# Value sums of a sampling pipeline moved from TensorE to VectorE, ten gather buffers, and a new product order in the attention that runs beside it

## What is computed

```python
v00, v01, v10, v11 = gather(y0i, x0i), gather(y0i, x1i), gather(y1i, x0i), gather(y1i, x1i)
out = v00 * (1 - wx) * (1 - wy) + v01 * wx * (1 - wy) + v10 * (1 - wx) * wy + v11 * wx * wy
...
attn = jnp.einsum('bgpc,bgpkc->bgpk', qh, k)      # layer 0: 9 samples k of a pixel p and group g
attn = jax.nn.softmax(attn, axis=-1)
out = jnp.einsum('bgpk,bgpkc->bgpc', attn, v)
...
logits = jnp.einsum('bhqd,bhkd->bhqk', q, k) * scale      # layer 1
attn = jax.nn.softmax(logits, axis=-1)
ctx = jnp.einsum('bhqk,bhkd->bhqd', attn, v)
```

## Time and profile before

| | |
|---|---|
| median of 3 runs | 10331.16 us (10326.96 to 10343.2) |
| the profiled execution | 10341.0 us, its span 10339.2 us |
| PE busy | 7631.7 us, 74% of the span |
| DVE busy | 5293.7 us, 51% |
| ACT busy | 3754.9 us, 36% |
| POOL busy | 5133.8 us, 50% |
| mean granted clock of TensorE | 0.858 of full speed |

### The profile page before, as it was taken

How to read it: one execution, slowest core, us unless ns; L and a number is a source line. 1 busy time by engine, 2 the same in 40 slices (tenths; PEclk the granted TensorE clock), 3 DMA queues, 4 the chain that set the end, 5 groups by cost and what they waited for, 6 DMA issues and landing times. The chain is left out here.

```text
span 10339.2 us, 94511 instructions
## 1 busy us (share of the span) xinstructions
PE 7631.7 (74%) x30870; PEld 3966.5 (38%) x30870; DVE 5293.7 (51%) x9576; ACT 3754.9 (36%) x5426; POOL 5133.8 (50%) x4768
## 2 busy tenths in 40 slices
PE   7623326654893799879999687978996999855894
PEld 3612213442442344334444233433442444333563
DVE  7555544564664566556666455656632666421003
ACT  2100002310561366526666244635663455400221
POOL 1078875676776677767777576767500000002003
PEclk9866667877896799979999888988998999966997
DMA  3854335675543555455454445545412111142223
GB/s 128 310 140 107 108 106 162 205 257 178 154 132 117 157 145 140 130 150 147 131 145 134 152 143 159 142 136 154 129 37 77 53 47 46 33 117 93 69 75 108
DMA packets 680981, 1331.69 MB, mean 129 GB/s; under 512 B 173223, under 2 KB 417980, under 8 KB 665376
## 3 DMA queue, kind: packets, MB, share of 16 engines
q0 software_dynamic: 229632, 631.22, 22.0%
q1 hardware_dynamic: 432480, 619.58, 19.5%
q10 hardware_dynamic: 18432, 75.51, 1.8%
HBM read 1018.55 MB, written 307.68 MB: 128 GB/s over the span
## 5 line engine op out<-in xcount | busy, mean ns | idle before, releaser
L660 POOL DMA_INDIRECT sa_slot<-s_table,sa_rec x4608 | 4942.4, 1073 | 2462.7 <-issue 1413.8
L1572 PE MATMUL a_ctx<-a_p,a_v 128*64 128x512 f32 x6400 | 1740.3, 622 | 177.6 <-issue 177.6
L1659 DVE CUSTOM_DVE_ANT_0 a_above<-a_late,a_above 128x512 f32<-128x512 f32 x1600 | 1105.6, 691 | 1449.9 <-PE a_late L1517 1381.0
L1591 ACT ACTIVATE a_p<-a_s 128x1024 f32<-128x1024 f32 x1600 | 1629.9, 1019 | 154.6 <-PE a_s L1555 154.0
L1600 ACT ACTIVATE a_above<-a_diff 128x512 f32<-128x512 f32 x1600 | 956.2, 598 | 1855.9 <-PE a_diff L1505 1820.1
L815 PE MATMUL sa_sums<-keep_ident,sa_vals 128*128 128x128 f32 x4608 | 711.5, 305 | 759.4 <-DVE sa_vals L758 759.4
L1505 PE MATMUL a_diff<-a_kd,a_q 96*128 96x512 f32 x1600 | 840.4, 525 | 277.7 <-DMA a_q<-s_q 256.0
L1555 PE MATMUL a_s<-a_q,a_k 98*128 98x512 f32 x3200 | 1042.6, 407 | 0.0
L815 PEld LDWEIGHTS sa_sums<-keep_ident,sa_vals 128*128 128x128 f32 x4608 | 581.5, 157 | 1171.7 <-DVE sa_vals L758 774.5
L706 DVE TENSOR_TENSOR sa_slot<-sa_slot,sa_q 128x1152 f32<-128x1152 f32 x512 | 693.5, 1354 | 613.7 <-DMA sa_slot<-s_table,sa_rec 613.7
L2155 POOL MEMSET x_ctx<- 128x2 f32 x2 | 0.2, 101 | 1802.2 <-POOLq L74 1802.2
(11 more groups left out here) (272 smaller groups left out, 7922.5 us busy)
## 6 DMA issues: line engine op xcount, KB each, us to landing
sa_slot<-s_table,sa_rec POOLq DMA_INDIRECT x4608
s_table<-t_rows ACTq DMA_DIRECT2D x64, 1024.0 KB, 7.5
a_q<-s_q SPq DMA_DIRECT2D x160, 384.0 KB, 4.4
s_part<-a_o SPq DMA_DIRECT2D x160, 256.0 KB, 2.5
t_qwin<-s_dwq SPq DMA_DIRECT2D x64, 512.0 KB, 6.0
t_kvwin<-s_dwkv SPq DMA_DIRECT2D x64, 386.0 KB, 12.1
a_kd<-s_kd SPq DMA_DIRECT2D x128, 192.0 KB, 4.1
a_o<-s_part SPq DMA_DIRECT2D x96, 256.0 KB, 2.7
```

Of the source, the lines that this page charges most:

```text
L660: pool.indirect_dma_start(out=self.slot[g][:, k, :, :, :].rearrange("p c a n -> p (c a n)"), out_offset=None, in_=self.s["table"][n // TIL ...
L1572: mm = pe.matmul(self.ps_ctx[i * 2 * HD:(i + 1) * 2 * HD, :], self.v_and_ones(run.head, kb), self.p[slot % P_SLOTS][:, i * CHUNK:(i + 1) * ...
L1591: act.activation(self.p[slot % P_SLOTS][:, :], self.ps_s[slot % 2], ACT.Exp, scale=float(HD) ** -0.5).then_inc(self.exped, 1)
L1659: dve.tensor_tensor_reduce(above, self.ps_late, above, 1.0, LOWEST, ALU.add, ALU.max, self.pair_max[:, t, j:j + 1]).then_inc(self.late_got, 1)
```

## The change

Three things are changed together.

- The value products stay on DVE but are written in place, over the values in the gather buffer. A new DVE instruction for each group (`add_values`) sums the 36 corner samples of 32 channels into `vals`, which is now [128, 128] for each half tile. It reads the samples with a pitch of 64 elements (256 bytes) as the inner step. PE keeps one transpose for each half tile (`turn_values`). A half tile becomes 19 pieces and a tile 38, so in slots 0 and up every slot has one piece; the tile rate of one in 38 slots is the same. `PROJECT_PIECES` goes from 33 to 42 (1.1 tiles either way).
- The eight gather buffers, bound to the groups, become ten in a ring. A buffer comes free after `add_values`. `HALF`, which also decides the list of each stage, is 19.
- In the attention, PE does the value products of two slots together in every odd slot, between the difference product and the late product; in even slots it does none. In odd slots the scores come ahead of the difference.

```diff
-PROJECT_PIECES = 33
+PROJECT_PIECES = 42
-HALF = 15
+HALF = 19
+    SLOTS = 10
-        self.slot = [r.sb(f"slot{g}", [P, K, 4, 2, HC]) for g in range(G)]
-        self.vals = r.sb("vals", [P, 4 * K, P])
+        self.slot = [r.sb(f"slot{u}", [P, K, 4, 2, HC]) for u in range(self.SLOTS)]
+        self.vals = [r.sb(f"vals{i}", [P, P]) for i in range(2)]
...
     def gather(self, pool, n, g):
         if g == 0:
             pool.wait_ge(self.tile_in[n % 2], 32 * (n // 2) + 32)
-        if n > 0:
-            pool.wait_ge(self.values_made, G * (n - 1) + g + 1)
+        turn, u = divmod(n * G + g, self.SLOTS)
+        if turn > 0:
+            pool.wait_ge(self.values_made, n * G + g - self.SLOTS + 1)
...
     def freed(self, j):
-        n, g = divmod(j, G)
-        return self.PIECES * (n - 1) + HALF * (g // 4) + 11 + g % 4
+        n, g = divmod(j - self.SLOTS, G)
+        return self.PIECES * n + HALF * (g // 4) + 12 + 2 * (g % 4)
...
+        elif m > 10 and m % 2 == 1:
+            self.weigh_values(dve, t, n, 4 * i + (m - 11) // 2)
         elif m > 10:
-            self.values(dve, n, 4 * i + m - 11)
+            self.add_values(dve, t, n, 4 * i + (m - 11) // 2)
...
+    def weigh_values(self, dve, t, n, g):
         i, j = divmod(g, 4)
-        if j == 0 and 2 * n + i > 0:
-            dve.wait_ge(self.values_summed, 2 * n + i)
-        v = self.slot[g][:, :, :, 1, :].rearrange("p k c n -> p (k c) n")
+        v = self.slot_of(n, g)[:, :, :, 1, :].rearrange("p k c n -> p (k c) n")
         w = self.corner[i][:, j * K:(j + 1) * K, :, :].rearrange("p k y x -> p (k y x)").unsqueeze(2)
-        dve.tensor_tensor(self.vals[:, :, j * HC:(j + 1) * HC], v, w.to_broadcast([P, 4 * K, HC]), ALU.mult)\
-            .then_inc(self.values_made, 1)
+        t.inc(dve.tensor_tensor(v, v, w.to_broadcast([P, 4 * K, HC]), ALU.mult))
+
+    def add_values(self, dve, t, n, g):
+        i, j = divmod(g, 4)
+        if j == 0 and n > 0:
+            dve.wait_ge(self.values_turned, 2 * (n - 1) + i + 1)
+        dve.wait_ge(self.chain, t.base + t.n)
+        dve.tensor_reduce(self.vals[i][:, j * HC:(j + 1) * HC], self.slot_of(n, g)[:, :, :, 1, :].rearrange("p k c n -> p n (k c)"),
+                          AX_X, ALU.add).then_inc(self.values_made, 1)
...
-    def sum_values(self, pe, n, i, part):
-        if part == 0:
-            pe.wait_ge(self.values_made, G * n + 4 * i + 4)
...
-        for j in range(part * step, (part + 1) * step):
-            mm = pe.matmul(self.ps_sum[i], self.vals[:, j, :], self.keep.ident[:, :],
-                           start=(j == 0), stop=(j == 4 * K - 1), is_transpose=True)
...
+    def turn_values(self, pe, n, i):
+        pe.wait_ge(self.values_made, G * n + 4 * i + 4)
...
+        pe.transpose(self.ps_sum[i], self.vals[i][:, :], self.keep.ident[:, :]).then_inc(self.values_turned, 1)
...
     def tensor(self, pe, slot):
-        self.diff_of_pair(pe, slot)
-        if 0 <= slot < self.slots:
-            self.weigh(pe, slot)
+        if slot % 2 == 0:
+            self.diff_of_pair(pe, slot)
+            if 0 <= slot < self.slots:
+                self.weigh(pe, slot)
+        else:
+            if 0 <= slot < self.slots:
+                self.weigh(pe, slot)
+            self.diff_of_pair(pe, slot)
+            for j in (slot - 3, slot - 2):
+                if 0 <= j < self.slots:
+                    self.sum_block(pe, j)
         self.late_of_pair(pe, slot)
         self.turn_shift(pe, slot)
-        if 0 <= slot - 2 < self.slots:
-            self.sum_block(pe, slot - 2)
```

More of the change, by code:

```diff
@@ L586, in __init__ @@
         self.const_in = r.sem("const_in")
-        self.gathered = [r.sem(f"gathered{g}") for g in range(G)]
+        self.gathered = [r.sem(f"gathered{u}") for u in range(self.SLOTS)]
         self.values_made = r.sem("values_made")
-        self.values_summed = r.sem("values_summed")
+        self.values_turned = r.sem("values_turned")
         self.logits_made = r.sem("logits_made")
@@ L656, in gather, with slot_of @@
             pool.wait_ge(self.tile_in[n % 2], 32 * (n // 2) + 32)
[L657 to L658 removed]
+        turn, u = divmod(n * G + g, self.SLOTS)
+        if turn > 0:
+            pool.wait_ge(self.values_made, n * G + g - self.SLOTS + 1)
         for k in range(K):
             pool.indirect_dma_start(
[L661 removed]
+                out=self.slot[u][:, k, :, :, :].rearrange("p c a n -> p (c a n)"), out_offset=None,
                 in_=self.s["table"][n // TILES].rearrange("t p (g n) -> (t p g) n", g=G),
                 in_offset=bass.IndirectOffsetOnAxis(ap=self.rec[n % 2][:, g * K + k:g * K + k + 1].bitcast(U32), axis=0),
[L664 removed]
+            ).then_inc(self.gathered[u], 16)
+    def slot_of(self, n, g):
+        return self.slot[(n * G + g) % self.SLOTS]
     def pool(self, pool, target):
@@ L701, in q_times_k @@
     def q_times_k(self, dve, t, n, g):
-        dve.wait_ge(self.gathered[g], 16 * K * n + 16 * K)
-        k = self.slot[g][:, :, :, 0, :].rearrange("p k c n -> p (k c) n")
+        turn, u = divmod(n * G + g, self.SLOTS)
+        dve.wait_ge(self.gathered[u], 16 * K * turn + 16 * K)
+        k = self.slot[u][:, :, :, 0, :].rearrange("p k c n -> p (k c) n")
         q = self.q[n % 2][:, g * HC:(g + 1) * HC].unsqueeze(1).to_broadcast([P, 4 * K, HC])
@@ L708, in scores @@
     def scores(self, dve, t, n, g):
-        k = self.slot[g][:, :, :, 0, :].rearrange("p k c n -> p (k c) n")
+        k = self.slot_of(n, g)[:, :, :, 0, :].rearrange("p k c n -> p (k c) n")
         dve.wait_ge(self.chain, t.base + t.n)
@@ L798, in tensor @@
             n, m = divmod(piece, self.PIECES)
-            if 1 <= m < 1 + self.PARTS and n >= 1:
-                self.sum_values(pe, n - 1, 1, m - 1)
+            if m == 1 and n >= 1:
+                self.turn_values(pe, n - 1, 1)
             if m == 8 and n >= 1:
                 self.project(pe, n - 1)
-            if HALF + 1 <= m < HALF + 1 + self.PARTS and n < B * TILES:
-                self.sum_values(pe, n, 0, m - HALF - 1)
-    def sum_values(self, pe, n, i, part):
-        if part == 0:
-            pe.wait_ge(self.values_made, G * n + 4 * i + 4)
-            if i == 1:
-                pe.wait_ge(self.outT_made, 2 * n + 1)
-            elif n > 0:
-                pe.wait_ge(self.x1_made, n)
-        step = 4 * K // self.PARTS
-        for j in range(part * step, (part + 1) * step):
-            mm = pe.matmul(self.ps_sum[i], self.vals[:, j, :], self.keep.ident[:, :],
-                           start=(j == 0), stop=(j == 4 * K - 1), is_transpose=True)
-        if part == self.PARTS - 1:
-            mm.then_inc(self.values_summed, 1)
+            if m == HALF + 1 and n < B * TILES:
+                self.turn_values(pe, n, 0)
+    def turn_values(self, pe, n, i):
+        pe.wait_ge(self.values_made, G * n + 4 * i + 4)
+        if i == 1:
+            pe.wait_ge(self.outT_made, 2 * n + 1)
+        elif n > 0:
+            pe.wait_ge(self.x1_made, n)
+        pe.transpose(self.ps_sum[i], self.vals[i][:, :], self.keep.ident[:, :]).then_inc(self.values_turned, 1)
     def project(self, pe, n):
```

4 lines of the change are left out of this document (1 added, 3 removed).

## The result

The changed kernel took 10388.16 us as a median (10376.5 to 10399.22), the kernel before 10331.16. The ratio is 1.0051, with a 95% interval of 1.0036 to 1.0066: slower by half a per cent, where 10080 us was predicted. Its profiled execution has a span of 10387.6 us against 10339.2.

The account below looks back on a forecast made before the run. PE ended last with POOL 3% behind; after the change POOL would end last. Savings 191 (attentions) + 48 + 12 (projections) + 12 (tables) - 13 (convolutions) = 250 us gave 10091, 10080 as a median; range 9990 to 10330.

Parts of the forecast that it names:

- Sums onto DVE: Eight new strided reductions a tile on DVE, taken at 1.35 us each, covered by PE's 2.15 us slot.
- Rival 2: Reduction about double, 2.70 us: attention's gain gone, 10275 us, or a worse PE wait with the same end; chance 0.17.
- rest of 12.0 us: Part of PE's attention tile for new runs, turned maxima and projection, beside 81.7 us of slots and 7.2 of transposes.
- The new order on PE: Attention: no gain or loss on slot pairs, 0.7 us saved per new run, 1.9 us a tile.
- The new wait on a pair: Attention: PE's next late product waits for DVE's maximum, 0.4 us on each pair of slots.
- POOL's cadence: Gathers stay at 1.364 us from one to the next, 98.2 us a tile.
- the stretch of 0.51 us a product: Gathers held by DVE's value products: 8.2 us a tile, 0.51 us for each product, expected to stay.
- one more group: Convolutions: POOL's list grows from 78 to 79 groups, 13 us lost.
- Ten buffers: Take away POOL's wait for buffers, 54.5 us in the largest stage; 10 us left at each stage's start.
- Projections: Transposes leave PE, 8 us in each of six stages, 48 us; 12 more for one group less in the third.
- The frame: Each attention stage takes the larger of POOL's gather list and PE's shortened chain; attentions save 191 us.
- The test named in advance: Signs of a wrong forecast: reduction mean over 1.6 us, late-product waits over 0.5 us a pair, cadence other than 1.36.

Follow-up runs that it names:

- e1: Changed kernel with the new reduction reading 1152 neighbouring elements, so sums of the wrong elements: 10178.12 us, ratio 0.9846 to the kernel before.
- e3: Kernel before with the new PE order alone, sums still on PE: 10253.08 us, ratio 0.9921.
- e10: Changed kernel with a ring of 8 buffers in place of 10: 10367.03 us, ratio 1.0026 to the kernel before.
- e2: Changed kernel with the attention's PE order of the kernel before: 10346.18 us, ratio 1.0009 to the kernel before.
- e11: Changed kernel with each sum made by two halving additions of whole rows and a reduction over 9: 10310.81 us, ratio 0.9968 to the kernel before.
- e18: Changed kernel with late product ahead of value products in every pair, a round's four products before its sums, and halving additions: 10215.49 us, ratio 0.9879.
- e15: Kernel before with the new PE order, but the late product ahead of the eight value products at or just before turns: 10369.14 us, ratio 1.0037.
- e13: Changed kernel with the late product ahead of the eight value products only at or just before turns: 10489.97 us, ratio 1.0151 to the kernel before.
- e16: Kernel before with value products in groups of eight and the late product ahead of them in every pair: 10180.83 us, ratio 0.9848.
- e17: Changed kernel with the late product ahead of the value products in every pair and a round's four products before its four sums: 10168.58 us, ratio 0.9833.

## Why the prediction was wrong, by its own steps

- **Sums onto DVE: this step failed.** I took 1.35 us out of 1.35 to 7.5, by the row nearest in operation and count. It was 2.131. The note that spoke against it, the Trainium skill's "SBUF — State Buffer", section "Door 1: The DMA port swizzle", had the direction right, and e1 isolates the step: same operation, same count, 1.349 us without it. That lines of 16 bytes are the reason is not shown, since no run tries a step in between. The step is worth 210 of the 308 us between forecast and result. I had written that nothing in the trace stands for a step that costs; true, and no reason to take the lower bound.
- **The rule by which a slower sum would be paid was wrong too.** Rival 2 counts DVE's work in a pair against PE's 4.30 us. For 2.13 us it gives 0.69 x 2 + 1.35 + 2.13 = 4.86, or 4.5 us a tile, which POOL's list would have hidden: no loss. In plain pairs that is about right: the median from one group of eight value products to the next is 4.6 us with a sum and 4.4 without. The loss is at the turns, in TensorE's waits and its clock (37 of the 47 us between the changed kernel and e1 in the largest stage), which the sum of the prediction lumped into a "rest of 12.0 us" and did not open.
- **The new order on PE.** Beside the old vector work it did what was counted: nothing on the pairs, and 0.7 us at each new run, some 90 us for the 128 runs of the seven stages. e3 gained 87. In its largest stage the waits at new runs fell by 45.0 - 25.5 = 19.5 us, 0.6 for each of 32 runs, of 21 us that the stage gained. The new wait on a pair was about 0.2 us, not 0.4; the 0.8 us of the prediction leaves out the late product's own 0.33, and 0.33 + 0.34 + 0.47 = 1.14 against 1.25 gives 0.1. What I didn't ask is what the order does once DVE is slow: it then loses 42 us.
- **POOL's cadence.** In the attentions it held: e1's largest stage had 882 gathers in 1215 us, 1.377 each, against 1.364. Elsewhere it failed: I kept the stretch of 0.51 us a product everywhere, but it depends on what DVE does between two products. In the convolutions it went from 7 to 53 us, and with the 13 us of one more group (right) it makes 59 of the 63.
- **Ten buffers.** Counted as the end of 54.5 us of waits; 51.5 remained, and e10 shows that the two buffers do nothing. The waits come with DVE's lateness: 16.5 us are left in e1, with the same ten buffers.
- **Projections.** 48 + 12 us expected, 6 came (15 in e1). I took the 18 transposes of the earlier trace rows as lying on PE's path because nothing stood between them, without reading the stage's own row. In the second projection stage PE was busy 84.30 of 154.70 us before. The view of after shows a transpose that waits for DVE's last sum in PE's queue:

```profile
2610.44 0.47 PE L824 MATMUL sa_sums<-keep_ident,sa_vals 128*128 128x128 f32 x1 [9.75 <-DVE sa_vals L772]
```

- **The frame held.** With the reduction at its assumed price the attentions saved 156 us of the 191, and the total is 10178: inside the range, 98 over the forecast. Of these, 45 are the projections, 35 the attentions (the second stage took 529 us, not 514: there TensorE still ended last, by 18 us), 8 the convolutions; the last 10 are the step from the profiled execution to the median, which the forecast took off and e1 does not show. Two numbers of the text are slips. The seven attention stages of the earlier trace rows with gathers sum to 4144 us, not 4414; no term rests on it. Its lists hold 315 groups for the attentions, 39.4 tiles and not 40.6, which moves the prices of the rivals by 3%.
- **The test named in advance** worked: a mean of the reduction over 1.6 us was the first of the signs that it would be wrong. TensorE's busy share of 83 to 88% told nothing: it is 86% in the changed kernel and 87% in e1.

Open: why the old order with the strided sum (e2) passes its turns in 15.38 us, faster than any other kernel here, was not tried apart. It has 1.12 us of idle TensorE there, at a granted clock of 1.00.

## What to carry to other kernels

When work moves onto an engine with an access pattern that no row of the profile shows, the forecast should be worked out at both ends, and the likely case should be the rule that speaks against, not the nearest row by name of operation. A spare of 0.1 us in a slot is no cover: ask who stands behind the longer instruction at the rare slots (turns, new runs), where waits of TensorE went with a lower clock. Instructions that disturb another engine's transfers are best put back to back, and a reordering of products is to be judged for all slots alike; a local repair of one pair was worse than none.

## What the runs showed of the hardware

- A DVE reduction of 1152 f32 with a step of 256 bytes took 2.131 us (changed kernel), with neighbouring elements 1.349 (e1): 1.85 against 1.17 ns an element.
- Halving additions with two inputs, 576 elements in 0.757 us and 288 in 0.458 (e11), with the reduction that ends them take less than the step (1.863 us in all), but hold up gathers as products do (e18); the reductions of 1152 elements do not, with the step or without it (gathers at 0.95 beside L772 in the convolutions of the changed kernel and of e1).
- Waits of 1.26 and 1.71 us on TensorE (changed kernel, e15) lie in stretches of 7.5 and 5.6 us at a mean granted clock of 0.77 and 0.70, in which eight value products took up to 3.45 us instead of 1.94. At those clocks 0.23 x 7.5 and 0.30 x 5.6 us are lost, 1.7 us each time (an estimate), beside the wait. Over 23 turns the mean clock was 0.91 to 0.92 where TensorE stood idle 3.03 and 2.29 us of a turn (e13, changed kernel), and 1.00 where it stood idle 0.30 to 1.36 (before, e2, e3, e16). That the idle time brings the clock down is what this order of the kernels suggests, with e17 (2.15 us, 0.99) against it; no run changes the one without the other.
